# Statistics of x2 moved from VectorE to ScalarE, and GpSimd's part at the end to VectorE, in an AdaLN layer

## Chip, cores, metric

One core of one Trainium2 chip. The metric is device time in microseconds (us), the median of several executions. TensorE (PE) multiplies matrices into PSUM; VectorE (DVE), ScalarE (ACT) and GpSimd (POOL) do the rest; SyncE (SP) and GpSimd issue the DMAs of the steady part.

## The reference

16 sequences of 512 rows of 256 float32. Each goes through an attention block and a routed feed-forward block, both modulated by rows computed from a condition vector:

```python
mod = (_silu(L0_c) @ L0_wmod).reshape(16, 6, 1, -1)          # sa, ca, ga, sb, cb, gb
h = _layernorm(x) * (1 + ca) + sa
x = x + ga * attention(h)            # softmax over |q.k| / 16, causal, then values and Wo
h = _layernorm(x) * (1 + cb) + sb
x = x + gb * ffn(h)
# ffn: scores against 8 cluster and 64 tile signatures, a piecewise linear gate,
# argmax of cluster and of tile in it, a small spline network of the picked tile
# whose scalar result times the tile's direction row is added to h; then layer norm
```

## The kernel before

The kernel works on pairs of sequences, p = 0 to 7, slots s = 0 and 1, and in each sequence on four row tiles of 128, t = 0 to 3. It is cut into three parts that run on different pairs at the same time:

- Part a and b, the attention: layer norm of x (statistics by VectorE), transposes (`XT`), key and value products (`G_`, `V_`), scores (`S_`), absolute value by ScalarE (`b_abs`), mask and row maximum by VectorE (`b_ttr`), exponential by ScalarE (`b_exp`), transposed probabilities (`PT_`, `b_pt`), values (`AT`), and the residual sum `b_x2` (line 2262) of VectorE, which makes x2.
- Part c, the second layer norm and the router. Here the work goes by groups: sequences 0 and 1 alone (groups 0 and 1), pairs 1 to 6 (groups 2 to 7), and sequences 14 and 15 alone (groups 8 and 9). Statistics of x2: `b_st` (line 2267) is one bn_stats of VectorE per row tile; `c_var` (lines 2192 to 2202) six tiny operations per group, in four calls, that make the variance; `c_gs` (lines 1255, 1256) a logarithm and an exponential of ScalarE; `c_nw` (lines 2207 to 2215) a Newton step of VectorE; `c_xh` (line 1316) the normalised row tiles by ScalarE, which TensorE turns (`HT`). Then `c_h2`, the scores `FS`, `c_fs`, `ecl`; the cluster gates and their argmax on VectorE (`clc`, `clb`, `pick`), ScalarE's `elo`, the tile gates and argmax (`loc`, `lob`), the one-hot rows (`oh`), `OHT`, the gather product `GA` and its copy `c_ga` (line 1377).
- The tail of a group: the spline network on VectorE (`spl`, eight calls; the last one, line 2396, makes the negative mean `nmu3` and marks `nmu_rdy`), the sum `y_` (line 2402, one input in PSUM, marks `y_rdy`), the squares `y_sq` by ScalarE (line 1385, with an accumulated sum), `y_var`, `y_gs`, `y_nw`, then `oa` (line 2422, both tensor inputs in SBUF) and `ob` (line 2436). For all groups but the last, the result of `ob` is added onto x2 in DRAM by a DMA that GpSimd issues (`ay`, line 2138). For the last group, `base` (line 2129) of GpSimd first makes x2 plus the shift row in two operations of 128x512, after the group's first `y_`, and `ob` adds onto that; SyncE sends the result.

GpSimd also makes the gated value matrices `ms(p, s)` (line 2120, 128x512, both inputs in SBUF). From pair 3 on it waits, besides what it needs, for the first `y_` of the group of sequence 2(p - 3).

Each engine runs its list in order; the lists at the end of each engine's function are written out call by call. Waits are semaphore waits at the head of each call. `BANK` gives each product one of the eight PSUM banks, and `free` makes TensorE wait for the last reader of the bank.

Of the kernel before, what the change touches and what calls it, by code (L numbers as in the profile page):

```python
# [8 lines left out]
ALU = mybir.AluOpType  # L9
# [37 lines left out]
def adaln_kernel(nc, ins, out):  # L47
# [26 lines left out]
    with ExitStack() as ctx:  # L74
# [3 lines left out]
        def sem(name):  # L78
# [43 lines left out]
        eps = sb("eps", [P, 1])  # L122
        xhat = [sb(f"xhat{s}", [P, NT, D]) for s in range(2)]
# [60 lines left out]
        consts_rdy, temp_rdy = sem("constants_ready"), sem("temperature_ready")  # L184
        ga_two, ga_own, ga_first = ([sem(f"{n}{b}") for b in range(2)] for n in ("ga_product_of", "ga_of", "ga_and_bias_of"))
# [21 lines left out]
        ln3_var, ln3_guess = sem("ln3_var"), sem("ln3_guess")  # L207
        nmu_rdy, sq_rdy = sem("negative_mean_ready"), sem("squares_ready")
# [81 lines left out]
        def _(spq):  # L290
# [95 lines left out]
            xo(0, 0)  # L386
            ldx(2, 1)
            xo(1, 0)
            ldga(3, 0)
            ldx(3, 0)  # L390
            ldga(3, 1)
# [3 lines left out]
            ldga(4, 0)  # L395
            ldx(4, 0)
            ldga(4, 1)
# [19 lines left out]
            for i in range(0, 2):  # L417
                ldga(7, i)
            ldgb(5, 0)
            ldx(7, 0)  # L420
# [20 lines left out]
        def _(pe):  # L441
# [106 lines left out]
            def su_gax(b):  # L548

                pe.wait_ge(in_mod_ga, 16)  # L550
                pe.wait_ge(cT_rdy, 1)
                mod_rows(free(f"su_gax{b}", (ga_own[b], 1)), 2, P,
                         lambda c: c_T[:, c, b:b + 1].broadcast_to([P, P])).then_inc(ga_two[b], 1)

            def su_ga():
                pe.wait_ge(in_mod_ga, 16)
                pe.wait_ge(cT_rdy, 1)
                mod_rows(free("su_ga", (ga_rows, 1)), 2, B, lambda c: c_T[:, c, :]).then_inc(ga_mod, 1)
# [13 lines left out]
            def su_gb():  # L572
                pe.wait_ge(in_mod2, 16)
                pe.wait_ge(cT_rdy, 1)
                mod_rows(free("su_gb", (gb_rows, 1)), 5, B, lambda c: c_T[:, c, :]).then_inc(gb_mod, 1)
# [128 lines left out]
            su_A()  # L704
            su_gax(1)
            su_gax(0)
            su_wo()
            for i in range(0, 2):
                XT(0, 0, i)
            su_ga()  # L710
            su_vb()
            su_bias()
            su_M()
            su_sig()
            for i in range(0, 2):
                G_(0, 0, i)
            XT(0, 1, 0)
            su_colf()
            for i in range(0, 2):
                V_(0, 0, i)  # L720
            XT(0, 1, 1)
            S_(0, 0, 0)
            V_(0, 0, 2)
            S_(0, 0, 1)
            PT_(0, 0, 0)
            S_(0, 0, 2)
            V_(0, 0, 3)
# [2948 lines left out]
```

## Time and profile before

| | us |
|---|---|
| median of 3 runs (lowest, highest) | 442.09 (441.46, 444.2) |
| the profiled execution's own time | 442.74 |
| its span, first to last instruction | 440.9 |
| busy in the span: PE, DVE, ACT, POOL | 398.2, 372.7, 334.3, 57.5 |

The profile's times are those of one execution; its own time is 1.8 us over its span and 0.65 us over the median. Matmuls are pipelined, so that a busy TensorE need not be one at its peak. Columns of the stretches and of the rows in order of time are named at the first group of each view.

### The profile page before, as it was taken

The page shows a single profiled execution, that of the slowest core. Times are in us where ns is not written, and L with a number is a line of the kernel's source. Part 1 is how long each engine was busy: PE and PEld are TensorE (multiplying, and loading weights), DVE is VectorE, ACT ScalarE, POOL GpSimd, SP SyncE. Part 2 cuts the span into 40 slices and gives each one's busy share as a digit, 9 for nine tenths or more (in the row PEclk, how much of TensorE's full clock was granted, in tenths as well). Part 3 has the DMA queues.
Part 4 walks back from the last instruction along what each step waited for, and adds up shares of the span by engine and source line. Part 5 has one row for each costly group of instructions (what it writes and reads, how often), then busy time and mean ns, then how long its engine had stood idle before and what let it go on. Part 6 is the DMA issues. An engine that isn't in the chain of part 4 may idle for free. (4 is left out here: it accounts for less than half of the span.)

```text
span 440.9 us, 8049 instructions
## 1 busy us (share of the span) xinstructions
PE 398.2 (90%) x2107; PEld 310.6 (70%) x2107; DVE 372.7 (85%) x1352; ACT 334.3 (76%) x796; POOL 57.5 (13%) x97
## 2 busy tenths in 40 slices
PE   8999999999999999999999999999899989867030
PEld 8776777768786878776977688777778677766020
DVE  4775757768787998899889999999899998998996
ACT  1344777877999599979988699789896886978541
POOL 4073040000020010210003000310022020001123
PEclk9999999999999999999999999999999999986655
DMA  6821174032103125164018610760055071004374
GB/s 227 240 60 25 30 189 120 0 121 76 45 0 119 33 76 88 27 158 128 1 46 172 141 25 10 184 166 2 25 96 97 26 141 52 0 3 71 48 119 96
DMA packets 33452, 36.19 MB, mean 82 GB/s; under 512 B 3402, under 2 KB 28992, under 8 KB 33408
## 3 DMA queue, kind: packets, MB, share of 16 engines
q1 hardware_dynamic: 25040, 27.15, 20.3%
q0 software_dynamic: 8064, 8.00, 13.0%
q10 hardware_dynamic: 304, 0.54, 0.3%
q8 instruction: 18, 0.29, 0.3%
q14 instruction: 26, 0.21, 0.2%
HBM read 19.36 MB, written 16.32 MB: 81 GB/s over the span
## 5 line engine op out<-in xcount | busy, mean ns | idle before, releaser
L636 PE MATMUL bank<-v,probsT 128*128 128x257 f32 x320 | 79.4, 383 | 1.6 <-ACT gath L1377 1.2
L619 PE MATMUL bank<-h,g 128*128 128x128 f32 (+3 forms) x256 | 78.7, 435 | 0.6 <-DVE x L2262 0.6
L636 PEld LDWEIGHTS bank<-v,probsT 128*128 128x128 f32 x320 | 57.5, 190 | 12.3 <-issue 2.6
L609 PE MATMUL bank<-m_ga,h 128*128 128x258 f32 x256 | 65.3, 383 | 0.8 <-DVE negmax L2250 0.7
L596 PE MATMUL bank<-h,a_sb 128*128 128x512 f32 x128 | 59.7, 594 | 0.0
L619 PEld LDWEIGHTS bank<-h,g 128*128 128x128 f32 x256 | 43.1, 190 | 16.6 <-issue 8.8
L609 PEld LDWEIGHTS bank<-m_ga,h 128*128 128x128 f32 x256 | 46.3, 191 | 12.0 <-issue 3.9
L2120 POOL TENSOR_TENSOR m_ga<-m_sb,a_row 128x512 f32<-128x512 f32 x16 | 21.6, 1359 | 222.5 <-DVE y L2402 184.5
L1385 ACT ACTIVATE gath<-y,nmu 128x256 f32<-128x256 f32 x64 | 32.0, 502 | 14.5 <-issue 10.8
L2250 DVE CUSTOM_DVE_ANT_0 probs<-bank,cmask 128x128 f32<-128x128 f32 (+1 forms) x64 | 30.8, 482 | 13.0 <-ACT bank L1292 13.0
L2138 POOL DMA_DIRECT2D out<-res x15 | 19.4, 1292 | 150.6 <-DVE res L2436 150.6
L1292 ACT ACTIVATE bank<-bank,v 128x128 f32<-128x128 f32 (+1 forms) x64 | 31.8, 496 | 9.3 <-PE bank L619 9.0
L2422 DVE SCALAR_TENSOR_TENSOR y<-y,nmu,gb_row 128x256 f32<-128x256 f32 x64 | 37.8, 598 | 0.5 <-issue 0.5
L1297 ACT ACTIVATE probs<-probs,negmax 128x128 f32<-128x128 f32 (+1 forms) x64 | 35.4, 558 | 2.4 <-DVE negmax L2250 2.2
L1316 ACT ACTIVATE wide<-x,nmr,rstd 128x256 f32<-128x256 f32 x64 | 34.8, 590 | 3.0 <-DVE nmr L2215 2.8
L1266 ACT ACTIVATE xhat<-x,nmr,rstd 128x256 f32<-128x256 f32 x62 | 35.3, 598 | 1.9 <-DVE nmr L2215 1.9
L596 PEld LDWEIGHTS bank<-h,a_sb 128*128 128x128 f32 x128 | 23.2, 190 | 18.7 <-issue 17.7
L1303 ACT ACTIVATE probsT<-bank 128x128 f32<-128x128 f32 (+1 forms) x64 | 27.4, 433 | 8.2 <-PE bank L627 8.2
L2262 DVE SCALAR_TENSOR_TENSOR x<-bank,rinv,x 128x256 f32<-128x256 f32 x64 | 30.6, 478 | 0.6
L2402 DVE SCALAR_TENSOR_TENSOR y<-gath,mag,bank 128x256 f32<-128x256 f32 x64 | 29.6, 472 | 1.4 <-DVE shift L2394 0.4
L1377 ACT ACTIVATE gath<-bank 128x322 f32<-128x322 f32 x64 | 25.8, 444 | 6.2 <-PE bank L689 6.0
L1276 ACT ACTIVATE h<-bank,sa_col,ca_col 128x512 f32<-128x512 f32 x31 | 23.8, 773 | 8.7 <-PE bank L584 8.7
(192 smaller groups left out, 818.4 us busy)
## 6 DMA issues: line engine op xcount, KB each, us to landing
x<-in_L_attn_x SPq DMA_DIRECT2D x16, 512.0 KB, 4.1
out<-x SPq DMA_DIRECT2D x15, 512.0 KB, 5.0
out<-res POOLq DMA_DIRECT2D x15, 512.0 KB, 6.1
gb_row<-gate_rows SPq DMA_DIRECT2D x16, 256.0 KB, 3.4
a_row<-gate_rows SPq DMA_DIRECT2D x14, 256.0 KB, 3.4
wide<-in_L_wmod SPq DMA_DIRECT2D x1, 768.0 KB, 8.0
wide<-in_L_wmod ACTq DMA_DIRECT2D x1, 512.0 KB, 5.8
out<-res SPq DMA_DIRECT2D x2, 256.0 KB, 2.2
```

The costliest lines, as they stand in the source:

```text
L596: last = mm(ps[:, 0:S], a_sb[:, c, m * P:(m + 1) * P], h[s][:, c, :], start=(c == 0), stop=(c == KC - 1))
L609: last = mm(ps[:, 0:VW], h[s][:, c, t * P:(t + 1) * P], m_ga[p % 2][s][:, c, :], start=(c == 0), stop=(c == KC - 1))
L619: last = mm(ps[:, 0:w], g[s][:, c, t * P:(t + 1) * P], h[s][:, c, 0:w], start=(c == 0), stop=(c == KC - 1))
L636: last = mm(ps[:, 0:D + 1], probsT[s][t][:, j * P:(j + 1) * P], v_sb[s][:, j, 0:D + 1], start=(j == 0), stop=(j == t))
L1266: A(xhat[s][:, t, :], x_sb[p % 2][s][:, t, :], ACT.Identity, bias=ln1["nmr"][:, i:i + 1], scale=ln1["rstd"][:, i:i + 1]).then_inc(xhat_rea ...
L1292: A(ps, ps, ACT.Abs, bias=v_sb[s][:, t, TCOL:TCOL + 1], scale=SCALE).then_inc(abs_rdy, 1)
L1297: A(probs[s][t][:, :], probs[s][t][:, :], ACT.Exp, bias=negmax[s][:, t:t + 1], scale=-1.0).then_inc(probs_rdy, 1)
L1316: A(xhat2[:, t, :], x2[p % 2][s][:, t % NT, :], ACT.Identity, bias=ln2["nmr"][:, i:i + 1], scale=ln2["rstd"][:, i:i + 1]).then_inc(xhat2_r ...
L1385: A(gath[:, t, PAR:GW], y[:, t, :], ACT.Square, bias=nmu3[g % 2][:, t:t + 1], accum_out=ln3["sq"][:, t:t + 1]).then_inc(sq_rdy, 1)
L2250: v.tensor_tensor_reduce(out=probs[s][t][:, :], in0=banks[BANK[f"S{s}{t}"]][:, 0:w], in1=cmask[:, S - w:S], scale=-1.0, scalar=0.0, op0=AL ...
L2262: stt(out=x2[p % 2][s][:, t, :], in0=banks[BANK[f"AT{s}{t}"]][:, 0:D], scalar=rinv[s][:, t:t + 1], in1=x_sb[p % 2][s][:, t, :], op0=ALU.mu ...
L2422: stt(out=y[:, t, :], in0=y[:, t, :], scalar=nmu3[g % 2][:, t:t + 1], in1=gb_row[g % 2][t // NT][:, 0, :], op0=ALU.add, op1=ALU.mult).then ...
```

## The change

Row statistics. A constant `BY_SQUARE = 5` divides the groups: from pair 5 on (groups 6 to 9, 24 row tiles) x2's statistics come in another way. `b_x2` also accumulates the row sum. `c_var(g, 0)` scales the sums to the negative mean, ScalarE squares each row tile with that as its bias and accumulates the squares (`c_sq`, new; it writes the squares over the tile that `c_xh` writes later), `c_var(g, 1)` makes the variance, and ScalarE takes the logarithm from the accumulated squares directly. All 24 `b_st` and the six tiny operations of these groups go; two tiny ones per group come.

```diff
+            def c_sq(g, t):
+                (p, s), i = of_group(g, t // NT), stat(g).start + t
+                act.wait_ge(x2_mean, g - group_of(2 * BY_SQUARE) + 1)
+                need(act, h2t_done, KC * user(g, t // NT))
+                A(xhat2[:, t, :], x2[p % 2][s][:, t % NT, :], ACT.Square, bias=ln2["nmu"][:, i:i + 1],
+                  accum_out=x2_sq[:, i:i + 1]).then_inc(x2_squared, 1)
...
             def c_gs(g):
-                ln_guess(ln2, stat(g), ln2_var, g + 1, act_ln2, ln2_guess)
+                if g < group_of(2 * BY_SQUARE):
+                    ln_guess(ln2, stat(g), ln2_var, g + 1, act_ln2, ln2_guess)
+                    return
+                guess = ln2["guess"][:, stat(g)]
+                act.wait_ge(x2_squared, NT * (before(g + 1) - 2 * BY_SQUARE))
+                need(act, ln2_ready, g)
+                act_ln2.link(act, A(guess, x2_sq[:, stat(g)], ACT.Ln, bias=eps[:, 0:1], scale=1.0 / D))
+                A(guess, guess, ACT.Exp, scale=-0.5).then_inc(ln2_guess, 1)
...
             def b_x2(p, s, t):
...
+                if p > BY_SQUARE:
+                    dve.wait_ge(x2_mean, group_of(seq(p - 1, s)) - group_of(2 * BY_SQUARE) + 1)
                 stt(out=x2[p % 2][s][:, t, :], in0=banks[BANK[f"AT{s}{t}"]][:, 0:D], scalar=rinv[s][:, t:t + 1],
-                    in1=x_sb[p % 2][s][:, t, :], op0=ALU.mult, op1=ALU.add).then_inc(x2_rdy, 1)
+                    in1=x_sb[p % 2][s][:, t, :], op0=ALU.mult, op1=ALU.add,
+                    accum_out=x2_sum[:, NT * s + t:NT * s + t + 1] if p >= BY_SQUARE else None).then_inc(x2_rdy, 1)
...
             def c_var(g, i):
+                n = g - group_of(2 * BY_SQUARE)
+                if n >= 0 and i == 0:
+                    dve.wait_ge(x2_rdy, NT * before(g + 1))
+                    need(dve, x2_squared, NT * (before(g) - 2 * BY_SQUARE))
+                    ts(ln2["nmu"][:, stat(g)], x2_sum[:, stat(g)], -1.0 / D, None, ALU.mult).then_inc(x2_mean, 1)
+                    return
+                if n >= 0:
+                    dve.wait_ge(x2_squared, NT * (before(g + 1) - 2 * BY_SQUARE))
+                    ts(ln2["var"][:, stat(g)], x2_sq[:, stat(g)], 1.0 / D, EPS, ALU.mult, ALU.add).then_inc(ln2_var, 1)
+                    return
```

GpSimd. The extra wait of `ms` is for the negative mean of that group and not for its first `y_`, and `base` is a function of VectorE:

```diff
                 if p > 2:
-                    pool.wait_ge(y_rdy, NT * seq(p - 3, 0) + 1)
+                    pool.wait_ge(nmu_rdy, group_of(seq(p - 3, 0)) + 1)
...
+            def base(g, u):
+                (p, s), t = of_group(g, u // 2), slice(2 * (u % 2), 2 * (u % 2) + 2)
+                dve.wait_ge(gb_ld[g % 2][u // 2], 16 * gb_uses(g, u // 2))
+                dve.wait_ge(x2_rdy, NT * seq(p, s) + 2 * (u % 2) + 2)
+                dve.wait_ge(summed[1], 16 * len(with_slot(range(BY_SUM), 1)))
```

At setup, the copies of the three gate products out of PSUM are calls of their own (`sd_gxc`, `sd_gac`, `sd_gbc`), which release the bank earlier; `BANK` gives another bank to `V00`, `G01`, `GA6`, `GA7` and to most setup products. All five lists are written anew: the same calls (but for those named) in another order. GpSimd's list has `ms(3, 1)` behind `ay(0, 0)`, and `ms(5, 1)` ahead of `ay(2, 1)`; `ms(7, 1)` stays behind `ay(4, 1)`. The end of VectorE's list:

```diff
-            for i in range(0, 2):
-                y_(9, i)
-            for i in range(2, 4):
-                ob(8, i)
-            y_(9, 2)
-            for i in range(0, 3):
-                oa(9, i)
-            y_(9, 3)
-            y_var(9, 0)
-            for i in range(0, 2):
-                y_nw(9, i)
-            oa(9, 3)
-            y_nw(9, 2)
+            for i in range(1, 3):
+                y_(9, i)
+            ob(8, 3)
+            oa(9, 0)
+            y_(9, 3)
+            for i in range(1, 3):
+                oa(9, i)
+            base(9, 0)
+            y_var(9, 0)
+            y_nw(9, 0)
+            base(9, 1)
+            for i in range(1, 3):
+                y_nw(9, i)
+            oa(9, 3)
             for i in range(0, 4):
                 ob(9, i)
```

ScalarE's list between the last exponential of the attention, `b_exp(7, 1, 3)`, and the first normalised tile of the last group, `c_xh(9, 0)`, was: `c_fs(8, 1)`, `ecl(8)`, ..., `c_ga(7, 0)` to `c_ga(7, 7)` with `elo(8)` in them, `c_gs(9)`, the table load, `tanh(7)`, `gelu(8)`. It is now: ..., `c_ga(7, 1)`, `c_sq(9, 0)`, `c_ga(7, 2)`, `c_sq(9, 1)`, `c_sq(9, 2)`, `elo(8)`, `c_sq(9, 3)`, `c_ga(7, 3)`, `c_ga(7, 4)`, `c_gs(9)`, the table load, `c_ga(7, 5)` to `c_ga(7, 7)`, `tanh(7)`; `gelu(8)` follows the `c_xh`.

## Rows read from the trace of the kernel before

**Rows 1.** The page: busy us (share) of each engine; by line, count, busy, mean ns.
```profile
PE 398.2 (90%) x2107; PEld 310.6 (70%) x2107; DVE 372.7 (85%) x1352; ACT 334.3 (76%) x796; POOL 57.5 (13%) x97
...
L2422 DVE SCALAR_TENSOR_TENSOR y<-y,nmu,gb_row 128x256 f32<-128x256 f32 x64 | 37.8, 598 | 0.5 <-issue 0.5
...
L1377 ACT ACTIVATE gath<-bank 128x322 f32<-128x322 f32 x64 | 25.8, 444 | 6.2 <-PE bank L689 6.0
```

**Rows 2.** Stretches: length, busy us (instructions) of PE, PEld, DVE, ACT, POOL; PE clock, DMA.
```profile
11.00:66.00 55.00, 55.00 (x270) 40.67 (x269) 35.55 (x134) 30.72 (x65) 17.78 (x30) 1.00 0.39 109
66.00:286.00 220.00, 218.10 (x1165) 169.35 (x1164) 190.37 (x697) 187.07 (x436) 16.83 (x13) 1.00 0.31 79
286.00:374.00 88.00, 84.63 (x461) 65.80 (x460) 81.27 (x282) 73.76 (x180) 9.01 (x7) 1.00 0.35 76
374.00:388.70 14.70, 13.28 (x89) 10.93 (x89) 14.51 (x52) 12.79 (x37) 0.00 (x0) 1.00 0.01 2
388.70:403.70 15.00, 10.61 (x51) 9.65 (x50) 13.14 (x61) 11.44 (x31) 1.28 (x1) 0.66 0.22 39
403.70:429.60 25.90, 7.19 (x32) 5.25 (x30) 25.33 (x96) 14.91 (x43) 3.84 (x4) 0.63 0.52 79
429.60:438.30 8.70, 0.00 (x0) 0.00 (x0) 7.50 (x14) 1.70 (x6) 3.77 (x3) 0.50 0.44 61
```

**Rows 3.** Order of time, the end: start, length, engine, line, tiles, xcount, [idle before].
```profile
428.20 0.51 ACT L1385 ACTIVATE gath<-y,nmu 128x256 f32<-128x256 f32 x1 [3.21 <-DVE y L2402]
...
428.70 0.49 ACT L1385 ACTIVATE gath<-y,nmu 128x256 f32<-128x256 f32 x1
...
429.60 4.45 DVE L2422 SCALAR_TENSOR_TENSOR y<-y,nmu,gb_row 128x256 f32<-128x256 f32 x3
...
430.37 3.00 POOL L2129 TENSOR_TENSOR res<-x,gb_row 128x512 f32<-128x512 f32 x2
433.98 0.47 DVE L2402 SCALAR_TENSOR_TENSOR y<-gath,mag,bank 128x256 f32<-128x256 f32 x1
...
435.16 0.17 DVE L2409 TENSOR_SCALAR var<-sq 128x4 f32<-128x4 f32 x1 [0.72 <-ACT gath L1385]
...
435.73 0.16 DVE L2207 TENSOR_TENSOR newt<-guess 128x4 f32<-128x4 f32 x1 [0.39 <-ACT guess L1394]
...
436.60 1.67 DVE L2436 SCALAR_TENSOR_TENSOR res<-y,rstd,res 128x256 f32<-128x256 f32 x4
```

**Rows 4.** VectorE by line and shape: count, busy us, mean ns, idle before.
```profile
L2262 DVE SCALAR_TENSOR_TENSOR x<-bank,rinv,x 128x256 f32<-128x256 f32 x64 | 30.6, 478 | 0.6
...
L2267 DVE BATCH_NORM_STATS2 st<-x 128x6 f32<-128x256 f32 x64 | 26.1, 416 | 0.3
...
L2305 DVE TENSOR_TENSOR seg<-cal,steps 128x448 f32<-128x448 f32 x12 | 7.4, 617 | 0.0
...
L2250 DVE DVE_READ_ACCUMULATOR2_ANT negmax<- 128x1 f32 x64 | 5.3, 82 | 0.0
...
L2202 DVE SCALAR_TENSOR_TENSOR var<-var,dif 128x8 f32<-128x8 f32 x13 | 2.1, 164 | 0.3
```

**Rows 5.** Order of time, 335 to 339 us: VectorE and GpSimd.
```profile
336.03 2.42 DVE L2422 SCALAR_TENSOR_TENSOR y<-y,nmu,gb_row 128x256 f32<-128x256 f32 x1
336.36 1.80 POOL L2120 TENSOR_TENSOR m_ga<-m_sb,a_row 128x512 f32<-128x512 f32 x1
```

**Rows 6.** Order of time from 386 us: the last group on its way to the router.
```profile
388.24 0.48 DVE L2262 SCALAR_TENSOR_TENSOR x<-bank,rinv,x 128x256 f32<-128x256 f32 x1
...
391.09 0.20 ACT L1256 ACTIVATE guess<-guess 128x4 f32<-128x4 f32 x1
...
391.31 1.28 ACT L1227 ACT_TABLE_LOAD   x1
...
393.08 2.06 ACT L1316 ACTIVATE wide<-x,nmr,rstd 128x256 f32<-128x256 f32 x4
...
403.71 0.18 DVE L2289 TENSOR_SCALAR z_cl<-z_cl 128x32 f32<-128x32 f32 x1 [1.46 <-ACT z_cl L1346]
```

More of the change, by code:

```diff
@@ L1212, in _ @@
                 GA(9, i)
-            for i in range(0, 2):
-                BT(9, i)
+            BT(9, 1)
         @block.scalar
@@ L1958, in _ @@
                 c_ga(6, i)
             b_pt(7, 0, 2)
-            c_ga(6, 7)
+            tanh(6)
+            for i in range(6, 8):
+                c_ga(6, i)
             b_pt(7, 0, 3)
@@ L2172, in _ @@
             ay(8, 0)
-            for i in range(0, 2):
-                base(9, i)
         @block.vector
@@ L2830, in _ @@
+            b_ri(2, 0, 3)
+            clb(2, 3)
+            b_x2(2, 0, 3)
+            y_var(0, 0)
             clb(2, 4)
             pick(2, 0)
+            b_ttr(2, 1, 2)
+            for i in range(0, 6):
+                spl(1, i)
+            y_nw(0, 0)
             spl(1, 6)
+            b_ri(2, 1, 0)
+            b_st(2, 0, 2)
+            oa(0, 3)
+            pick(2, 1)
+            b_ttr(2, 1, 3)
+            a_st(4, 0, 0)
+            b_x2(2, 1, 0)
+            b_st(2, 0, 3)
+            y_nw(0, 1)
@@ new lines, in _ @@
+            b_st(4, 0, 1)
+            ob(2, 2)
+            b_ri(4, 0, 3)
+            b_ttr(4, 1, 2)
+            spl(3, 7)
+            b_x2(4, 0, 2)
+            ob(2, 3)
+            y_(3, 0)
+            clc(4, 9)
+            b_x2(4, 0, 3)
+            ob(2, 4)
+            clb(4, 0)
+            y_(3, 1)
+            for i in range(1, 3):
+                clb(4, i)
+            oa(2, 7)
+            ob(2, 5)
+            b_ri(4, 1, 0)
+            b_st(4, 0, 2)
+            b_x2(4, 1, 0)
@@ new lines, in _ @@
+            b_v(5, 1, 3)
+            for i in range(6, 8):
+                clc(5, i)
+            b_ri(5, 0, 1)
+            for i in range(0, 7):
+                spl(4, i)
+            b_x2(5, 0, 1)
+            b_ri(5, 0, 2)
+            b_x2(5, 0, 2)
+            spl(4, 7)
+            clc(5, 8)
+            ob(3, 4)
+            y_(4, 0)
+            b_ttr(5, 1, 2)
+            clc(5, 9)
+            b_ri(5, 0, 3)
+            y_(4, 1)
+            clb(5, 0)
+            ob(3, 5)
+            b_ri(5, 1, 0)
@@ new lines, in _ @@
+            oa(4, 2)
+            b_x2(6, 0, 0)
+            b_v(6, 1, 1)
+            for i in range(0, 2):
+                a_nw(7, i)
+            y_nw(4, 2)
+            a_nw(7, 2)
+            for i in range(0, 2):
+                ob(4, i)
+            b_ttr(6, 0, 3)
+            b_v(6, 1, 2)
+            clc(6, 0)
+            oa(4, 3)
+            clc(6, 1)
+            b_ttr(6, 1, 0)
+            a_nw(7, 3)
+            for i in range(2, 4):
+                clc(6, i)
+            oa(4, 4)
@@ new lines, in _ @@
+            clc(8, 8)
+            b_ri(7, 1, 3)
+            clc(8, 9)
+            b_x2(7, 1, 3)
+            clb(8, 0)
+            c_var(9, 0)
+            clb(8, 1)
+            y_var(6, 0)
+            clb(8, 2)
+            oa(6, 4)
+            clb(8, 3)
+            oa(6, 5)
+            clb(8, 4)
+            y_nw(6, 0)
+            pick(8, 0)
+            y_nw(6, 1)
+            pick(8, 1)
+            y_nw(6, 2)
+            oa(6, 6)
+            ob(6, 0)
+            for i in range(0, 2):
+                loc(8, i)
```

3037 lines of the change are left out of this document (1465 added, 1572 removed), and 14 rows, old and new, of the table BANK.

## The prediction

> **What bounds the kernel now.** I read the page first, then the busy time by stretches, then the order of time around the stretch where the bound changes and at the end. The page has TensorE busy 398.2 of 440.9 us, VectorE 372.7, ScalarE 334.3 [rows 1]; an average over two regimes. The stretches part them [rows 2]. From 11 to 66 us TensorE is busy without a gap (55.00 of 55.00), from 66 to 286 us for 218.10 of 220, from 286 to 374 us for 84.63 of 88: it sets the pace there, VectorE having 20 and 30 us to spare in the first two. In the 14.7 us up to 388.7 VectorE is full (14.51) and TensorE no more (13.28). At 388.24 VectorE starts the last row tile of x2 [rows 6]; from there the kernel is VectorE's: 13.14 of 15.0, 25.33 of 25.9, 7.50 of 8.7 us busy, while TensorE falls to 10.61, 7.19 and 0 us [rows 2] (its granted clock falls with that, from 1.00 to 0.66, 0.63 and 0.50 of full speed; the change leaves that as it is). So an edit ahead of 374 us counts only as far as TensorE waits less, and one behind 388 us counts in full on VectorE. From 388.24 to the end of VectorE's last instruction, 436.60 + 1.67 = 438.27, it is 50.0 us.
>
> **The sum is made against the profiled execution's own 442.74 us** (span 440.9), 0.65 us above the median of 442.09.
>
> **1. Setup and the new order up to pair 4: 0.** The number of TensorE instructions doesn't change, only their order, and it has no gap from 11 to 66 us [rows 2]: a bank released earlier can't make it start earlier. From 66 to 286 us it has 1.9 us of gaps in all, the most to win; a worse order could lose about as much. Bounds: -2 to +2.
>
> **2. `base` on VectorE: -3.1.** At the end three `oa` take 4.45 us, where three in a row without a hindrance are 1.28 (four `ob` take 1.67, so 0.40 from start to start, and 0.48 for the last) [rows 3]. The hindrance is GpSimd's two `base` operations, 430.37 to 433.37: the `oa` doesn't end before them, and the last `y_` starts at 433.98 [rows 3]. 4.45 - 1.28 = 3.17 us of stall go. The cost: two sums of 128x512 on VectorE. Nearest row: 128x448 with two inputs in 617 ns [rows 4], so 617 x 512 / 448 = 0.70 each as a length and some 0.62 from start to start. Before, 433.98 to 438.27 is 4.29 us, with idle times of 0.72 and 0.39 us in it, for the last squares and the exponential [rows 3]. After: `y_` 0.40, two `oa` 0.80 (they stood ahead of `y_` before), `base` 0.62, `y_var` 0.10, `y_nw` 0.10, `base` 0.62, the rest of the Newton step 0.5, `oa` 0.40, four `ob` 1.67: 5.2 us, 0.8 of which has only been moved; the exponential is there 1.3 us after `y_` ends, under 0.80 + 0.62. So 4.4 against 4.3: the sums cost 0.1 net. Bounds: -3.2 (sums free) to -1.8 (both in full).
>
> The Trainium skill ("SBUF — State Buffer", section "SBUF: two separate sides") says that GpSimd and a VectorE instruction with two SBUF inputs hold their common port pair for a whole instruction, and that the loser blocks fully. The trace agrees: 3.17 us of stall beside 3.00 us of GpSimd. The same rule makes a rival of the next item.
>
> **3. `ms` released by the negative mean: 0.** In the middle, too, a GpSimd product holds VectorE: an `oa` takes 2.42 us, 0.48 without, beside `ms` at 336.36 [rows 5]. All 64 `oa` take 598 ns in the mean [rows 1]: (598 - 480) x 64 = 7.6 us too much, 3.2 of it the end, so 4.4 us from pair 3 on, besides smaller operations. But this lies ahead of 374 us, where TensorE sets the pace. The new signal comes one call ahead of the old. In the new list `clb` and `ob` (two SBUF inputs) mostly stand close behind it, with `y_` among them; `ms(7, 1)` hangs on its `ay` as before. I take 0. Bounds: -1.5 to +1.5.
>
> **4. Statistics of x2, up to the last x2: -1.5.** VectorE loses 24 `bn_stats` of 416 ns [rows 4], some 0.37 from start to start: 8.9 us. It gains 24 accumulator reads of 82 ns (the only such rows are those of the row maximum) [rows 4]: 2.0. Six tiny operations become two in four groups: 16 x 0.16 = 2.6 us at most, half of it where they overlap. Net some 8 us, all but one `bn_stats` and one group's variance ahead of the last x2. What is in line then? Only in the 14.7 us ahead of 388.7 is VectorE full, with TensorE short of 1.4 us; from 286 to 374 us TensorE misses 3.4 us [rows 2]. So 4.8 us is the most that TensorE can win by, not 8. Against it, ScalarE gets 24 squares of 0.50 us from start to start, the read of the sum included (428.20 to 428.70) [rows 3]: 12.0 us, 20 of them (10.0) ahead of the last x2, eight in a row between the scores of pair 7. From 286 to 388.7 us ScalarE is busy for 73.76 + 12.79 = 86.6 of 102.7 us [rows 2], then 96.6. It keeps 6 us of 16, and exponentials and copies on which TensorE waits stand behind the squares. I take a third of what can be won. Bounds: -4.8 to +10.0, the whole load passed on.
>
> What the accumulated sum adds to `b_x2` (478 ns [rows 4]) no row shows but by that read of 82 ns; below 0 is excluded, since the operation stays. A sentence of the Trainium skill speaks against it: "Vector Engine (DVE) Microarchitecture Reference", section "7. Points that are easy to get wrong", has scalar_tensor_tensor with two float32 SBUF sources halve its throughput for want of a port for the accumulator. `b_x2` has one source in PSUM, and no run here shows the case; by that rule applied all the same, 24 x 0.27 = 6.5 us would come to VectorE and item 4 would be 0.
>
> **5. Statistics and order behind the last x2: +0.6.** On VectorE one `bn_stats` and the tiny operations go (-0.7), three `clb` of about 0.16 come behind this point (+0.5). The last group's chain gets longer. Before, x2 ends at 388.72, the exponential at 391.29, 2.6 us on; then the table load of 1.28; `c_xh` starts at 393.08, 4.4 us behind x2 [rows 6]. After: mean 0.3; four squares 2.0; between them `c_ga` four times at 0.37 (444 ns long [rows 1]) and `elo` 0.3; logarithm and exponential 0.4; table 1.3; three more `c_ga` 1.1 and `tanh` 0.2: 7.1, some 2.7 us later. VectorE waited 1.46 us at 403.71 for this chain [rows 6]. The new list gives it 65 calls in place of 58 between x2 and `clc(9, 0)`, ten coming, seven of them of 0.4 us (2.8) and three `clb` (0.5), three going (0.7): 2.6 more. That covers the 2.7. But these calls are then missing between `clc(9, 0)` and `loc(9, 0)` (24 in place of 35), where `elo(9)` must come back from ScalarE: +0.8 for both. -0.7 + 0.5 + 0.8 = +0.6. Bounds: -1 to +4.
>
> **Sum:** 442.74 + 0 - 3.1 + 0 - 1.5 + 0.6 = 438.7 us; less the 0.65 by which that execution was above the median: **438.1 us**, 0.9% under 442.09.
>
> **Rivals.**
> (a) ScalarE becomes the bound (the other side). For: it keeps 6 idle us of 102.7, its list is in order, and blocks of four to eight squares stand between calls of the attention. Against: a new order was written around them, and part of ScalarE's idle time was waiting for TensorE (`c_ga` alone 6.0 us [rows 1]). If three quarters of the 10.0 us pass to the last x2, that is +7.5 in place of -1.5: 447.1 us. It decides from the point where the last x2 starts more than 2.5 us behind 388.2: the remaining gains (3.1 - 0.6) are then used up.
> (b) VectorE held TensorE all along from pair 5, and the relief comes through: the last x2 4.8 us earlier, and a chain hidden behind `clb` and `y_` (item 5 at -0.2): 438.1 - 3.3 - 0.8 = 434.0 us. For: VectorE full in the last 14.7 us. Against: only 1.4 us of TensorE idle there.
> (c) The change doesn't do what it says with GpSimd: the products, released one call earlier, now meet two-input operations every time, all ten from pair 3 on, for some 1 us each. That is 10 us of VectorE in place of 4.4 and more; where half of the excess reaches TensorE, +3: 441 us. This is the port rule of the skill's SBUF page applied to the new list: `y_` reads PSUM and could pass, `clb` and `ob` can't.
>
> **Chances.** The forecast's own case (434.5 to 442) 0.60; (a) 0.13; (b) 0.15; (c) 0.12. For 8 times in 10 the range takes in (b), (c) and the edge of (a): 433.5 to 443.5 us. A measurement of this kernel tells about 1%, 4.4 us, from no change: faster by more (under 437.7) is (b) and half of the forecast's case, 0.45; slower by more (over 446.5) most of (a), 0.11; within 1%, 0.44.
>
> **What would show it.** Right: in the last 10 us no `oa` over 0.5 us, GpSimd without a tensor operation behind 374 us, two operations of about 0.65 us on VectorE ahead of `y_var` and within the Newton step; the last x2 starting between 384 and 389 us; from there to VectorE's end 47 to 48 us in place of 50.0 (50.0 - 3.1 + 0.6 = 47.5). ScalarE some 12 us busier, VectorE some 10 less (8, 3.2 of stall, less 1.4 for the sums). Wrong: the last x2 behind 391 us with ScalarE full from 286 us on (rival a), an idle time of over 3 us before `clc(9, 0)` or `loc(9, 0)` (item 5), `b_x2` of 0.7 us or more (the sum isn't free), `oa` or `clb` of over 1 us at each `ms` in the middle with a TensorE gap behind it (rival c).

## The result, and the profile after

The changed kernel takes **447.74 us** (median of 4 runs, 446.10 to 448.45), the kernel before beside it 442.31 (441.46 to 444.20). The ratio is 1.0114, 95% interval 1.0087 to 1.0141: slower by 5.4 us. The forecast was 438.1, the range ended at 443.5, and slower had a chance of 0.11. The profiled execution has a span of 446.1 us, a mean granted clock of 0.949 and a time of its own of 447.87.

The page of after, its first lines: busy time and share of each engine, then the busy tenths of TensorE and its granted clock in 40 slices.

```profile
PE 403.4 (90%) x2107; PEld 311.1 (70%) x2107; DVE 363.7 (82%) x1338; ACT 346.3 (78%) x844; POOL 55.4 (12%) x95
...
PE   8899999999999998999999999999989998888330
...
PEclk9989999999999999999999999999989999995855
```

Against [rows 1] VectorE is 9.0 us less busy and ScalarE 12.0 more, almost as forecast (10 and 12). What the forecast doesn't have: TensorE is 5.2 us *more* busy with the same 2107 products, and its clock row dips at the third and the thirtieth digit, where it had 9 before. By stretch, in the columns of [rows 2], the last edges moved to the new places of the same events:

```profile
11.00:66.00 55.00, 52.94 (x242) 37.10 (x240) 32.93 (x125) 27.67 (x59) 10.24 (x13) 0.97 0.30 89
66.00:286.00 220.00, 216.09 (x1159) 167.74 (x1160) 188.04 (x687) 186.03 (x433) 23.38 (x30) 1.00 0.31 79
286.00:374.00 88.00, 83.08 (x440) 63.60 (x439) 73.50 (x256) 78.84 (x203) 10.36 (x8) 0.98 0.39 81
374.00:397.40 23.40, 21.94 (x134) 17.83 (x131) 21.60 (x85) 20.79 (x62) 0.00 (x0) 1.00 0.07 24
```

In the first stretch TensorE had not one gap; now it misses 2.1 us and runs 242 products in place of 270. The loss begins there. From 286 to 374 us VectorE now has 14.5 us to spare (6.7 before), and TensorE is no better off for it (83.08 busy, 84.63 before).

A convenient ruler is the start of the last x2 tile of each pair. Before, they start at 67.1, 105.6, 150.9, 196.8, 245.3, 291.2, 339.3 and 388.2 us. After, they come later by 5.3, 4.8, 4.2, 7.7, 6.0, 7.0, 8.2 and 8.7 us, and the last output sum by 5.1. So 5.3 us are lost before pair 0 is done, 3.5 in pair 3, some 2.7 from pair 5 on, and 3.6 are won behind the last x2. (Below, "x2 late by" is this ruler against the kernel before.)

The end of after in order of time, VectorE, answers to [rows 3]:

```profile
396.91 0.47 DVE L2281 SCALAR_TENSOR_TENSOR x<-bank,rinv,x 128x256 f32<-128x256 f32 x1
...
439.43 0.68 DVE L2233 TENSOR_TENSOR res<-x,gb_row 128x512 f32<-128x512 f32 x1
440.04 0.16 DVE L2440 TENSOR_SCALAR var<-sq 128x4 f32<-128x4 f32 x1
440.30 0.16 DVE L2216 TENSOR_TENSOR newt<-guess 128x4 f32<-128x4 f32 x1
440.44 0.69 DVE L2233 TENSOR_TENSOR res<-x,gb_row 128x512 f32<-128x512 f32 x1
...
441.73 1.66 DVE L2467 SCALAR_TENSOR_TENSOR res<-y,rstd,res 128x256 f32<-128x256 f32 x4
```

The two sums take 0.68 and 0.69 us (0.70 was worked out), the last `oa` take 0.48, and from the last x2 to VectorE's end it is 441.73 + 1.66 - 396.91 = 46.5 us (47.5 forecast, 50.0 before). This half of the prediction holds; the first 370 us don't.

The start. First before, the two copies `h` and the first key products `G_` (line 596 before, 605 after), from VectorE, ScalarE and TensorE:

```profile
17.43 0.81 DVE L2460 TENSOR_SCALAR h<-bank,ca_col,sa_col 128x512 f32<-128x512 f32 x1
```

```profile
17.89 0.76 ACT L1276 ACTIVATE h<-bank,sa_col,ca_col 128x512 f32<-128x512 f32 x1
```

```profile
20.95 3.27 PE L596 MATMUL bank<-h,a_sb 128*128 128x512 f32 x7
```

Then after, TensorE, ScalarE and VectorE in the order of time of each:

```profile
18.03 0.60 PE L593 MATMUL bank<-ident,xhat 128*128 128x128 f32 x4
18.46 1.86 PE L490 MATMUL bank<-c_T,wide 128*128 128x16 f32 x16
21.84 3.36 PE L605 MATMUL bank<-h,a_sb 128*128 128x512 f32 x4 [1.52 <-ACT h L1279]
```

```profile
17.81 0.20 ACT L1259 ACTIVATE guess<-guess 128x4 f32<-128x4 f32 x1
20.32 0.60 ACT L1269 ACTIVATE xhat<-x,nmr,rstd 128x256 f32<-128x256 f32 x1 [2.31 <-DVE nmr L2224]
20.83 0.76 ACT L1279 ACTIVATE h<-bank,sa_col,ca_col 128x512 f32<-128x512 f32 x1
```

```profile
20.21 0.81 DVE L2491 TENSOR_SCALAR h<-bank,ca_col,sa_col 128x512 f32<-128x512 f32 x1
```

The first key product, `G_(0, 0, 0)`, needs both copies `h`. ScalarE stands idle for 2.31 us ahead of its own, in front of an x-hat tile of the *other* sequence that needs that sequence's Newton step, and VectorE's copy stands behind the same step; before, the copies started at 17.43 and 17.89 us. TensorE waits 1.52 us. Behind the wait the four instructions of this key product take 3.36 us, 0.84 each; undisturbed ones of this line 0.47 to 0.49. By stretches (same columns), the granted clock is 0.50 there, the lower of the two levels, 1.2 GHz:

```profile
20.00:22.00 2.00, 0.48 (x4) 0.41 (x4) 1.97 (x7) 1.68 (x3) 0.00 (x0) 0.82 0.22 46
22.00:24.00 2.00, 2.00 (x3) 0.97 (x4) 1.93 (x7) 0.08 (x1) 0.71 (x1) 0.50 0.08 8
```

and again from 325 us, behind a wait of 1.39 us for a copy of ScalarE. The additional busy time has two parts: up to the last x2 TensorE is busy 3.1 us longer than before, with these two stretches in it; the other 2.0 us lie behind the last x2 (19.8 beside 17.8), where it runs 93 instructions in place of 83 and the clock is low in both kernels.

And the gate product `ms(3, 1)`. Before, GpSimd makes it in one row with `ms(3, 0)`, ahead of the output DMA `ay(0, 0)`:

```profile
124.23 2.54 POOL L2120 TENSOR_TENSOR m_ga<-m_sb,a_row 128x512 f32<-128x512 f32 x2 [60.71 <-DVE y L2402]
163.98 1.41 POOL L2138 DMA_DIRECT2D out<-res  x1 [37.20 <-DVE res L2436]
```

After, around 168 us, GpSimd, VectorE and TensorE, each in order of time:

```profile
167.40 1.41 POOL L2149 DMA_DIRECT2D out<-res  x1 [36.91 <-DVE res L2467]
168.32 1.81 POOL L2140 TENSOR_TENSOR m_ga<-m_sb,a_row 128x512 f32<-128x512 f32 x1
```

```profile
167.59 2.57 DVE L2201 TENSOR_TENSOR dif<-st 128x8 f32<-128x8 f32 x1
```

```profile
171.59 1.20 PE L667 MATMUL bank<-f_sb,wide 128*128 128x137 f32 x8 [0.96 <-DVE negmax L2267]
```

`ms(3, 1)`, at about 125.5 us before, now stands behind `ay(0, 0)`, which waits until 167.4 us. It starts 43 us later and collides with VectorE: an operation of 128x8 with two inputs, elsewhere 0.17 us, takes 2.57 and ends 0.03 us behind the product. The 0.96 us that TensorE waits there are for a row maximum of VectorE, which that operation held up. The values `V` that need the product come 4.5 to 10.8 us later than before.

### The profile page after: what moved, and what is told of

Its sections match the earlier page's. It is cut to its first block and busy times, and to the rows that moved or that the text cites. A ratio compares the mean times of both kernels' runs of the same rounds, so it can differ in the third digit from the quotient of the medians.

```text
span 446.1 us, 8127 instructions
## 1 busy us (share of the span) xinstructions
PE 403.4 (90%) x2107; PEld 311.1 (70%) x2107; DVE 363.7 (82%) x1338; ACT 346.3 (78%) x844; POOL 55.4 (12%) x95
## 5 line engine op out<-in xcount | busy, mean ns | idle before, releaser
L645 PEld LDWEIGHTS bank<-v,probsT 128*128 128x128 f32 x320 | 58.8, 192 | 12.6 <-issue 4.2
L605 PE MATMUL bank<-h,a_sb 128*128 128x512 f32 x128 | 61.4, 606 | 1.5 <-ACT h L1279 1.5
L1403 ACT ACTIVATE gath<-y,nmu 128x256 f32<-128x256 f32 x64 | 32.1, 506 | 12.6 <-issue 6.5
L2140 POOL TENSOR_TENSOR m_ga<-m_sb,a_row 128x512 f32<-128x512 f32 x16 | 22.8, 1464 | 136.4 <-DVE nmu L2427 87.4
L2261 DVE TENSOR_TENSOR v<-bank,a_row 128x258 f32<-128x258 f32 x64 | 26.7, 419 | 14.4 <-PE bank L618 14.3
L2467 DVE SCALAR_TENSOR_TENSOR res<-y,rstd,gb_row 128x256 f32<-128x256 f32 x60 | 33.3, 569 | 0.0
```

The source lines that it names most:

```text
L605: last = mm(ps[:, 0:S], a_sb[:, c, m * P:(m + 1) * P], h[s][:, c, :], start=(c == 0), stop=(c == KC - 1))
L645: last = mm(ps[:, 0:D + 1], probsT[s][t][:, j * P:(j + 1) * P], v_sb[s][:, j, 0:D + 1], start=(j == 0), stop=(j == t))
L1403: A(gath[:, t, PAR:GW], y[:, t, :], ACT.Square, bias=nmu3[g % 2][:, t:t + 1], accum_out=ln3["sq"][:, t:t + 1]).then_inc(sq_rdy, 1)
L2467: stt(out=res[:, t, :] if g < BY_SUM else rest, in0=y[:, t, :], scalar=ln3["rstd"][:, t:t + 1], in1=rest, op0=ALU.mult, op1=ALU.add).then_ ...
```

## The experiments

All kernels stand against the kernel before, measured on the same chip beside them (441.9 to 442.3 us).

**e1: `base` alone.** The kernel before; `base(9, 0)` and `base(9, 1)` leave GpSimd's list for VectorE's, in the new order of the last calls.

```diff
-            for i in range(0, 3):
-                oa(9, i)
+            oa(9, 0)
             y_(9, 3)
+            for i in range(1, 3):
+                oa(9, i)
+            base(9, 0)
             y_var(9, 0)
-            for i in range(0, 2):
+            y_nw(9, 0)
+            base(9, 1)
+            for i in range(1, 3):
                 y_nw(9, i)
             oa(9, 3)
-            y_nw(9, 2)
```

> The kernel before with one part of the change: `base` on VectorE and the new order of the last sixteen calls. Theory (the stall of 3.17 us at the end is GpSimd's alone and the sums hide in the waits for the squares): 3.1 us faster than before, 439.2 us beside 442.3, no `oa` over 0.5 us in the last 10 us. Rival (what was held up waits for something else, or the sums cost in full): 440.5 to 442.3 us.

439.29 us (438.86 to 440.02), ratio 0.9942, interval 0.9928 to 0.9955: 2.7 us faster. x2 is where it was, within 0.2 us, at all eight pairs; from its last start to VectorE's end it is 46.7 us in the profile, 50.0 before. Item 2 holds.

**e2: the start of before.** The changed kernel, lists and setup banks of before to the end of pair 0.

> The changed kernel with the lists and the setup banks of before up to the end of pair 0, then its own lists. Theory (most of the loss arises in the setup: x2 of pair 0 ends 5.3 us later, with 1.5 us of TensorE idle and its clock halved from 21 to 25 us): x2 of pair 0 at 67 to 68 us again, the whole 443 to 444 us in place of 447.7. Rival (the loss comes later in any case, since the new lists of the middle are bound elsewhere): 446.5 us or more.

445.61 us (445.02 to 447.14), ratio 1.0089, interval 1.0070 to 1.0108: between the theory's range and the rival's. x2 late by -0.1 at pair 0, but by 3.5 at pair 1: at the seam TensorE waits 1.24 us for `v` and 1.20 for `h`, since the work with which the new order covers these waits had already been done. A seam has a price of its own.

**e3: `ms(3, 1)` ahead of `ay(0, 0)`.** The changed kernel with one call moved.

```diff
-            ms(3, 0)
+            for i in range(0, 2):
+                ms(3, i)
             ay(0, 0)
-            ms(3, 1)
```

> The changed kernel with GpSimd's product ms(3, 1) ahead of the DMA ay(0, 0) again, as before the change. In the changed kernel it starts at 168 us in place of 125, and pair 3's x2 falls from 4.2 to 7.7 us behind. Theory (late product, late values): 1 to 3 us faster than the changed kernel, 445 to 446.7 us. Rival (the 3.5 us come from VectorE's or TensorE's new order): 447.2 to 448.2 us.

445.00 us (443.50 to 446.94), ratio 1.0073, interval 1.0046 to 1.0099: 2.7 us back by the medians, but the ranges of the two kernels' runs overlap, and by the ratios it is 1.8. The profiles say about the same: from pair 2 to pair 4 the lateness of x2 grows by 1.8 us in the changed kernel and by 0.1 here (3.1, 2.7, 3.0, 4.8, 3.1 ... 4.2). The wait of 0.96 us is gone, and the values come 2.9 us earlier. This profiled execution, with a wait of 1.39 us at the start, has no half-speed stretch there, so that part of the 5.3 us at pair 0 comes and goes with the clock.

**e4: no squares.** The changed kernel with `bn_stats` in all groups, each one call behind its x2.

> The changed kernel with x2's statistics by bn_stats of VectorE again in all groups: no squares on ScalarE, no accumulated sums, 24 bn_stats one call behind their x2, the variance where the negative mean was; all else, the lists included, as changed. Theory (ScalarE's 12 us of squares cost more than VectorE's 8 us give): 1 to 3 us faster than the changed kernel, 445 to 446.7 us. Rival (the squares pay or are neutral): 447.5 to 452 us. By the forecast's item 4 it would be 1.5 us slower, 449.

450.22 us (449.38 to 453.66), ratio 1.0203, interval 1.0169 to 1.0236. In the new order the squares save 2.5 us against `bn_stats` at places that I chose. So rival (a) doesn't explain the loss: without its squares the kernel is slower, not faster, and in the changed kernel x2 is already 6.0 us late at pair 4, before the first square is made. What the squares cost ScalarE in this order is not told apart by this run, since VectorE gets its `bn_stats` back.

**e5: e2 and e3 together.**

> The changed kernel with two edits together: the order of before (and its setup) up to the end of pair 0, as in e2, and ms(3,1) ahead of ay(0,0) in GpSimd's list, as in e3. Theory A, the two losses are apart and add (e2 took about 2.3 us back, e3 about 2.6): 447.7 - 4.9 = 442.8 us, within 1 of it, and the last x2 of pair 4 stands 2 us or less behind that of before. Theory B, they are one loss seen at two places (a late start that ms(3,1) only hands on): 445 us, no better than e2 or e3 alone.

444.37 us (443.60 to 445.63), ratio 1.0052. Between the two: 0.6 us under e3. x2 late by -0.3, then 3.3: the seam again.

**e6: before's order to the end of pair 4, then the changed kernel's,** squares and all.

> The order of before up to the end of pair 4, and from there the changed kernel's: squares and accumulated sums for pairs 5 to 7, base by VectorE, gate products released by the negative mean. Theory A, the loss lies only in the new order of setup and pairs 0 to 4, and the squares are worth the 2.5 us that taking them away cost in e4: 439.3 (e1) - 2.5 = 436.8 us, 436 to 438.5, with the last x2 of pair 4 where before has it (within 0.5 us). Theory B, the squares only repay a delay that the new order itself made, and are worth nothing behind the old order: 439.3, within 0.7. Theory C, the lists behind pair 4 lose as well: 441 or more.

441.06 us (440.15 to 443.21), ratio 0.9987, interval 0.9968 to 1.0007. That is theory C: x2 late by 1.2 to 1.4 us from pair 3 on, the second normalisation by 3.8 to 4.6, and 1.8 us over e1. But 6.7 us of the changed kernel's time go with the order ahead of this cut.

**e7: squares in before's order.** e1 with the squares, each group's directly ahead of its `c_gs`.

```diff
+            for i in range(0, 8):
+                c_sq(6, i)
             c_gs(6)
```

> The kernel before with base by VectorE (e1) and, as the only further edit, squares and accumulated sums for x2 in pairs 5 to 7, in the order of before: each square stands directly ahead of the centre column's next ScalarE step. Against e1 (439.3 us) it prices the squares alone. Theory A, VectorE's relief comes through: 437 us, 436 to 438.5. Theory B, ScalarE's 24 more operations eat it: 439.3 to 441. Against e6 it tells whether the new order behind pair 4 gives anything: same time, no; e6 faster by over 1 us, yes.

452.68 us (451.00 to 454.80), ratio 1.0232, interval 1.0198 to 1.0266: 13.4 us over e1. Around 292 us VectorE waits at `c_var(6, 1)` for the eight squares, and TensorE for VectorE:

```profile
297.66 0.17 DVE L2309 TENSOR_SCALAR var<-x_sq 128x8 f32<-128x8 f32 x1 [4.64 <-ACT wide L1318]
```

```profile
299.51 1.97 PE L627 MATMUL bank<-h,g 128*128 128x512 f32 x2 [2.87 <-DVE v L2272]
```

x2 is late by 0.3 to pair 5, 5.2 in pair 6, 12.6 in pair 7: 4.9 us with the eight squares of group 6, 7.4 with the twelve of groups 7 and 8. ScalarE is 77% busy over the whole; the eight squares stand in one block, 293.58 to 297.6 us, that VectorE waits for.

**e8: the signal of `ms` alone,** in the kernel before.

```diff
-                    pool.wait_ge(y_rdy, NT * seq(p - 3, 0) + 1)
+                    pool.wait_ge(nmu_rdy, group_of(seq(p - 3, 0)) + 1)
```

> The kernel before, where GpSimd's gate product waits for the negative mean in place of the signal it waited for, and nothing else is changed. The prediction had it at 0 within 1.5 us. Theory A: 442.0, within 0.7, since the products start at the same place behind the two-input operations ahead of them. Theory B, later starts make them collide with VectorE more and hold the next step: 443 or more. Theory C: earlier by 1 us or more, since the product no longer runs against the copies.

442.51 us (441.37 to 443.65), ratio 1.0015, interval 0.9997 to 1.0032: no difference. In the order of before, item 3 holds.

**e9: squares about zero.** As e7, but each square waits for its tile alone, stands where it comes and writes to a buffer of its own; the variance is the mean square less the squared mean.

```diff
-                act.wait_ge(x2_mean, g - group_of(2 * BY_SQUARE) + 1)
+                act.wait_ge(x2_rdy, NT * before(g) + t + 1)
...
-                A(xhat2[:, t, :], x2[p % 2][s][:, t % NT, :], ACT.Square, bias=ln2["nmu"][:, i:i + 1],
+                A(sq_out[:, k % 2, :], x2[p % 2][s][:, t % NT, :], ACT.Square,
                   accum_out=x2_sq[:, i:i + 1]).then_inc(x2_squared, 1)
```

> The kernel before with base by VectorE (e1), and squares for x2 in pairs 5 to 7 as in e7, but taken about zero in place of the mean: each square waits only for its own tile and stands where the tile comes; the variance then needs the negative mean squared and subtracted, four small VectorE operations a group as before. The sums are otherwise the same. Theory A, what cost 13 us in e7 is that all eight squares of a group wait for the mean and stand in one block of 4 us between the last x2 and the next normalisation: without it 439.3 (e1) less what VectorE gains, 437 to 439.5 us. Theory B, it is ScalarE's added work itself (24 times 0.60 us): 445 or more, the last x2 5 us or more behind that of e1.

439.37 us (439.19 to 440.06), ratio 0.9944, interval 0.9923 to 0.9964. Theory A: e7's 13.4 us are gone with 24 squares as before. Whether the spreading does it or the missing wait for the mean, the two runs don't tell apart; a square that waits for the mean can't be spread over the tiles. And no more than that: e1 takes 439.29. VectorE's relief buys nothing in the order of before.

**e10: as e6, cut at the end of pair 2.**

> As e6, but the order of before only up to the end of pair 2; from there the changed kernel's lists. e6 (cut at pair 4's end) took 441.1 us, e5 (cut at pair 0's end, ms(3,1) early) 444.4. Theory A, the rest of the loss lies in pairs 3 and 4 of the new order: 443.5 to 444.5. Theory B, it lies in pairs 1 and 2 or at the seam of the cut itself: 441 to 442.

441.30 us (440.76 to 442.43), ratio 0.9983. Theory B, and within 0.3 us of e6: pairs 3 and 4 of the new order cost no time that can be seen, given that `ms(3, 1)` comes early, which it does here.

**e11: the new start alone.** The changed kernel's setup and pair 0, then e1.

> The reverse of e2: the changed kernel's order of the setup and of pair 0, then the order of before with base by VectorE at the end (e1) and no squares. Against e1 (439.3 us) it prices the new start alone. Theory A, the start costs what its 3.1 us at the last x2 of pair 0 show, and nothing behind takes it back: 442.4, 441.5 to 444 (more when TensorE's gap at 20 us lowers the granted clock). Theory B, the new start has only put work of pair 1 ahead of that x2 and gets the time back: 439.3 to 440.3.

444.83 us (442.25 to 447.13), ratio 1.0063, interval 1.0038 to 1.0088: 5.5 us over e1. x2 is late by 3.9, 3.8, 3.8, 4.0, 4.0, 3.7, 4.1 and 4.1 us: what the start loses nothing gives back. The runs spread over 4.9 us: three of 442.3 to 442.7 have a mean clock of 0.964 to 0.968, four of 446.1 to 447.1 have 0.953. The profile is of one of the fast ones and has no half-speed stretch ahead of the last x2; where the slower runs lose their time isn't shown.

**e12: two calls of the start moved,** on e3: `XT(0, 0, 1)` directly behind `XT(0, 0, 0)`, `a_h(0, 0, 1)` ahead of the gate rows.

> e3 (ms(3,1) early, 445.0 us) with two calls of the start moved: TensorE makes the second half of the first transposes directly behind the first, and VectorE's copy a_h(0,0,1), which TensorE waited 1.5 us for at 20.3 us, stands ahead of the gate rows. Theory A, that wait is the loss at the start: last x2 of pair 0 at 68.5 to 69.5 us (70.2 in e3), time 443 to 444. Theory B, other waits of the new start are late as well: no more than 0.5 us earlier at that x2, 444.5 or more.

445.47 us (444.07 to 449.13): theory B. The wait has only moved:

```profile
18.06 1.10 PE L496 MATMUL bank<-wide,c_T 128*128 128x256 f32 x4 [2.26 <-DVE h L2491]
```

The changed table of banks has `su_gax0` in the bank of `XT01`; the gate product now waits until the transposes are copied.

**e13: the new setup, pair 0 in before's order,** the rest as e11.

> As e11 (new start, then the order of before with base by VectorE, no squares; 444.8 us, x2 3.8 us late), but the changed kernel's order only up to the first two score products (G_(0,0,1)); pair 0 itself and all behind it in the order of before. Theory A, the setup's order is the loss: last x2 of pair 0 3 us or more behind e1, time 442.5 to 445. Theory B, the order of pair 0 (the setup's last products pulled apart, attention of sequence 1 later) is the loss: at most 1.5 us behind at that x2, time 439.5 to 441.

443.92 us (442.27 to 444.63), x2 late by 3.4, then 3.3 to 3.7. Theory A by its numbers, but the trace has a wait of 1.44 us, at 29.67 us, that my seam had made.

**e14: e6 with squares about zero,** guess and Newton steps earlier.

> e6 (order of before to the end of pair 4, then the changed kernel's; 441.1 us) with squares about zero as in e9: each waits for its own tile and stands where that comes; guess and Newton steps stand earlier, directly behind the last square of the group. Theory A, the 1.8 us that e6 lies above e1 are the squares' wait for the mean, by which the second normalisation comes 3.8 to 4.6 us late: 439.3, within 0.7, and TensorE's waits for wide and h (0.6 + 1.3 + 0.5 + 1.3 us in e6) shrink by half or more. Theory B, the order behind pair 4 itself is slower: 440.5 or more. A time under 438.6 would make it the fastest of all.

443.03 us (442.77 to 444.36), 2.0 over e6. Theory B by its number, but not by its reason, since this is slower than e6, too: x2 is late by 4.0 and 4.9 in pairs 6 and 7, where e6 has 0.9 and 1.4. My places for them in that list are worse than the list's own, and the run doesn't say which call is to blame.

**e15: e13 without its seam's wait.**

> As e13 (new setup, order of before from pair 0 on, base by VectorE, no squares; 443.9 us), with the seam mended: ScalarE makes all four x-hat tiles of sequence 1 ahead of the copy of the signatures, so that the 1.44 us wait of TensorE at 29.7 us goes. Theory A: last x2 of pair 0 at 68.5 to 69.7 us (2 us behind e1's 66.9, its waits of 0.45 and 1.71 us), time 441.5 to 442.7. Theory B, the order of the setup costs elsewhere too: 70 us or later, 443 or more.

443.02 us (440.96 to 443.82), ratio 1.0012: 3.7 over e1, and theory B by its numbers; x2 late by 3.4 with a half-speed stretch from 21.5 us in its profile. Three runs with a mean clock of 0.960 took 441.0 to 441.4. The setup's order is most of e11's loss.

**e16: e15 with a bank of its own for `su_gax0`,** and e12's two calls.

> e15 with the gate product su_gax(0) in a bank of its own, the second half of the first transposes directly behind the first, and VectorE's copy a_h(0,0,1) ahead of the gate rows (the order that e12 tried without the bank). Theory A, the shared bank and the late transposes are the setup's price: TensorE waits less than 0.5 us before 30 us, last x2 of pair 0 within 0.7 us of e1's 66.9, time 439.3 to 440.3. Theory B, the wait is for the input tiles or VectorE's list instead: no gain over e15, 441 or more.

442.64 us (441.43 to 443.88). Theory B by its numbers: TensorE still waits 1.92 us, at 21.94, now for `h` of ScalarE alone, since VectorE's copy is made at 17.60.

**e17: the same three edits on e3.**

> The changed kernel with ms(3,1) early (e3, 445.0 us) and the three edits of e16. e12, without the bank, took 445.5. Theory A: last x2 of pair 0 2 us earlier than in e3 (68.2 in place of 70.2), time 442.5 to 443.5, with less spread, since TensorE's wait at the start is gone. Theory B: 444.5 or more.

445.07 us (443.06 to 447.00). Theory B: a wait of 1.22 us for the same copy.

**e18: and `a_h(0, 0, 0)` ahead of `a_xh(0, 1, 0)` in ScalarE's list,** as it stood before.

```diff
-            a_xh(0, 1, 0)
             a_h(0, 0, 0)
-            a_xh(0, 1, 1)
+            for i in range(0, 2):
+                a_xh(0, 1, i)
```

> e17 (445.1 us) with one more call moved: ScalarE's copy a_h(0,0,0) stands ahead of the x-hat tile a_xh(0,1,0), as in the kernel before. Theory A, that order was what held TensorE at 20 us all along: no idle time before the first score product, no half-speed stretch behind it, last x2 of pair 0 at 69 us or earlier (73.5 in e17's profile, 70.2 in e3's), time 442 to 443.5 with a spread under 2 us. Theory B, the next wait (input, gate rows) takes its place: within 0.7 us of e17.

**442.63 us** (442.30 to 444.71), ratio 1.0019, interval 1.0006 to 1.0033: 2.4 under e17. Its start, ScalarE and TensorE in order of time, and the last x2 of pair 0:

```profile
17.91 0.76 ACT L1279 ACTIVATE h<-bank,sa_col,ca_col 128x512 f32<-128x512 f32 x1
```

```profile
18.28 1.85 PE L490 MATMUL bank<-c_T,wide 128*128 128x16 f32 x16
19.98 1.96 PE L605 MATMUL bank<-h,a_sb 128*128 128x512 f32 x4
21.87 2.10 PE L496 MATMUL bank<-wide,c_T 128*16 128x256 f32 x8
```

```profile
69.11 0.48 DVE L2281 SCALAR_TENSOR_TENSOR x<-bank,rinv,x 128x256 f32<-128x256 f32 x1
```

No wait, 0.49 us an instruction, and x2 at 69.11 in place of 72.38 in the changed kernel. Theory A, but for 0.1 us at that x2 and a spread of 2.4. e12, e16 and e17 had VectorE's copy early and left ScalarE's late, and gained nothing or little in time. ScalarE's call alone, without the other moves, wasn't tried: in the changed kernel VectorE's copy is as late as its own (20.21 beside 20.83 us), so little could come of it.

## Why the prediction was wrong

**Where the 5.4 us come from.** From differences of medians: `base` on VectorE -2.7 (e1); `ms(3, 1)` behind `ay(0, 0)` +2.7 (changed kernel against e3; 1.8 by ratios and traces); the first key product's wait and what the clock takes behind it +2.4 (e17 against e18); order and squares from pair 5 on +1.8 (e6 against e1). e18 less e1 less these 1.8 leaves 1.5 more in the new order of setup and attention; x2 of pair 0 is still 2.0 us late in e18, with 0.8 us of TensorE's idle time in it. The sum is 5.7, against 5.4 measured, but that is no check: the 1.5 is what was left over and has no experiment of its own. The runs of one kernel spread over 1 to 5 us, so each of these parts is uncertain by a microsecond or so. The firmest number is the direct one: with before's order to the end of pair 4 (e6) the changed kernel takes 6.7 us less.

**Item 1 is the step that failed** ("Setup and the new order up to pair 4: 0"). That TensorE has no gap from 11 to 66 us, so that a bank released earlier can't make it start earlier, is right, and it bounds the gain only. For the loss I wrote "about as much" as the 1.9 us of gaps. Nothing carries that: how much an order can lose is not read from the gaps of the old one, but from the distance between each call and its inputs. I had the new lists and all the times of before. ScalarE's `h` was started at 17.89 us and the key product at 20.95; the new list puts a call between them that needs the Newton step, ready at 20.93 before. The key product could no longer come at 20.95. Nor did I ask when `ay(0, 0)` ends (over 160 us) as I put `ms(3, 1)` behind it: in the diff that is one line that changes places. In place of 0 within 2, item 1 measured about +6.6 (2.7 + 2.4 + 1.5; 6.7 by e6).

**Item 2 was right**: -3.1 said, -2.7 measured by the medians and -3.3 behind the last x2 in e1's profile, the parts as worked out.

**Item 3 was right as far as it went.** The signal costs nothing (e8). GpSimd's products still meet VectorE, only at other operations: `oa` is down to 477 ns in the mean, 598 before, while `ob` is up to 569, 478 before.

```profile
L2467 DVE SCALAR_TENSOR_TENSOR res<-y,rstd,gb_row 128x256 f32<-128x256 f32 x60 | 33.3, 569 | 0.0
```

But the item weighed only the signal and not the place in the list.

**Item 4 didn't bring its gain.** -1.5 was a third of 4.8 us. Where squares replace `bn_stats` and the order is kept, it is 0 in one form (e9) and +13.4 in the other (e7). In the new lists behind pair 4 it is +1.8 (e6, which has the new order as well); only against `bn_stats` put into those same lists do the squares save 2.5 (e4). VectorE does fall by what was said, and TensorE takes none of it in e6 and e9: from 286 to 389 us it waits 3.4 us for ScalarE and 1.2 for VectorE in the trace of e1, 5.3 and 1.0 in that of e6. The accumulated sum itself is free but for its read:

```profile
L2281 DVE SCALAR_TENSOR_TENSOR x<-bank,rinv,x 128x256 f32<-128x256 f32 x64 | 30.4, 478 | 0.6
...
L2281 DVE DVE_READ_ACCUMULATOR x<-bank,rinv,x 128x1 f32 x24 | 2.0, 82 | 0.0
```

478 ns with 24 of 64 accumulating, as in [rows 4] with none, and 82 ns a read, as estimated. The sentence of the Trainium skill that the prediction sets against it ("Vector Engine (DVE) Microarchitecture Reference", section "7. Points that are easy to get wrong") halves the throughput with two SBUF sources; here, with one of the two in PSUM, the trace shows no halving.

**Item 5:** +0.6 said. From the last x2 to VectorE's end it is 46.5 us in the changed kernel and 46.7 in e1, which has `base` alone; so about -0.2 measured, within its bounds.

**The rivals.** (a) gave 447.1 us and comes near the time for the wrong reason: x2 is late before the first square is made, e4 is slower without them, and ScalarE isn't full from 286 us to the last x2 (99.6 of 111.4 us). That its number was near is luck. Its mechanism exists, though, and e7 prices it: some 5 us where eight squares stand in a block behind the mean. (b) falls: x2 is not earlier. (c) is not settled: its sign is in the trace (an `ob` of 3.16 us at 238.37 beside `ms` at 238.2, and the operation of 2.57 us at 168 with 0.96 us of TensorE behind it), but e8 prices the signal at 0 only in the order of before, and in the new lists no run takes it away. No rival had a start that gets worse. My list of "what would show it" looked from 286 us on, where ScalarE is full; the first sign is in the slices of the first 30 us.

**A version that beats both** is e1 at 439.29 us, 0.6% under the kernel before; e9 at 439.37 is its equal. Of the change, only the last residual sums are worth having.

## What to carry to other kernels

When a diff rewrites the order of calls, walk the new lists with the old times: for each call on an in-order engine, when are the inputs of those ahead of it there? A call of another sequence ahead of a ready one, or a gate product behind an output DMA, costs what its input lacks, here more where the clock fell, and an engine without a gap has no slack that could take it up. The gaps of the old order bound the gain and say nothing about the loss. And relief for one engine is worth nothing until the trace shows the bounding engine waiting for it; the work that pays for the relief is to be judged by where it stands, not by the idle share of its engine (13.4 us in e7, 0 in e9).

## What was unexpected of the hardware

The granted clock of TensorE falls to half in the middle of a busy stretch. In the changed kernel it is 0.50 from 22 to 24 us, at a wait of 1.52 us, and again from 325 us behind one of 1.39 us; e16, with 1.92 us, shows 0.57 from 20 to 28 us, and e15 has 0.50 from 22 to 24 us behind a wait of no more than 0.57; e18, without the wait, shows none at the start, and the kernel before shows none at all up to 390 us. Nor does it follow from the wait's length: the profiles of e3, e11, e12 and e13 have waits of 1.39, 1.29, 2.26 and 1.71 us at about the same place and no fall. The second place says it more plainly: every one of the twenty profiles has that wait, 1.34 to 1.53 us between 313 and 326 us, ahead of the same gather product, and the clock falls at it in three of them (the changed kernel, e14 and e18). What decides it stays open. So a short wait costs itself and, in some executions, about as much again: the four instructions of the first key product took 3.36 us in place of 1.96.

A square with a bias read from a tile takes 501 ns for 128x256 in the changed kernel, one without a bias 414 ns in e9; the read of the sum behind it 194 and 196 ns:

```profile
L1313 ACT ACTIVATE wide<-x,nmu 128x256 f32<-128x256 f32 x24 | 11.9, 501 | 0.6 <-DVE nmu L2294 0.6
```

```profile
L1321 ACT ACTIVATE sq_out<-x 128x256 f32<-128x256 f32 x24 | 9.9, 414 | 3.8 <-DVE x L2307 3.8
```
